# Four scheduling edits in the fourth layer of a four-layer attention stack

## What is computed

```python
zxbcdt = _rms(x, norm_w) @ in_proj_w
z, xBC = zxbcdt[..., :D_INNER], zxbcdt[..., D_INNER:D_INNER + CONV_DIM]
dt = jax.nn.softplus(zxbcdt[..., -H_M:] + dt_bias)
xBC = jax.nn.silu(conv_b + sum((padded[:, k:k + L, :] * conv_w[:, k] for k in range(D_CONV))))
xh, Bm, Cm = ...                       # 8 heads of 64, states of 128
def step(h, inp):                      # over the 112 tokens
    dec, u, bt, ct = inp
    h = h * dec[:, :, None, None] + u[..., None] * bt[:, None, None, :]
    return h, jnp.einsum('bhpn,bn->bhp', h, ct)
y = ys + D_skip[None, None, :, None] * xh
h = x + _rms(y * jax.nn.silu(z), gnorm_w) @ out_proj_w
q, k, v = _ln(h) @ Wq, enc @ Wk, enc @ Wv                    # 8 heads of 32
p = jax.nn.softmax(where(pad_mask, -1e9, q @ k.T / sqrt(32)))
out = h + (p @ v) @ Wo
```

## Time and profile before

| | us |
|---|---|
| median of three runs | 3705.43 |
| the profiled execution | 3712.93 |
| its span, first to last instruction | 3711.1 |
| the fourth layer within it, from 3106 on | 605 |
| TensorE busy over the span | 3461.5 |
| mean granted TensorE clock over the span | 0.966 of full |

### The profile page before, as it was taken

One profiled execution on the slowest core, in us unless ns is written; L12 is line 12 of the kernel. 1 busy time (PEld: TensorE's weight loads), 2 busy tenths in 40 slices (PEclk: granted clock), 3 DMA queues, 4 the chain that ended last, 5 costly groups with the idle time before them and its releaser, 6 DMA issues. The chain is left out here.

```text
span 3711.1 us, 67817 instructions
## 1 busy us (share of the span) xinstructions
PE 3461.5 (93%) x21748; PEld 2540.5 (68%) x21748; DVE 1933.5 (52%) x5863; ACT 1853.4 (50%) x5421; POOL 404.5 (11%) x488
## 2 busy tenths in 40 slices
PE   8999999999988999999979999999999997888888
PEld 6778778778866666666656766667667664555665
DVE  3654644654544444444544544544554545566656
ACT  3543544544445555555545555545545552444444
POOL 2101101101101111111010000000000001112111
PEclk9999999999998999999989999999999997898999
DMA  6000000000004000000010000000000000000000
GB/s 204 4 12 15 4 12 15 4 12 15 4 21 131 14 13 13 13 8 5 13 53 8 9 8 15 9 8 15 8 8 14 9 3 14 22 16 13 13 26 5
DMA packets 58462, 75.11 MB, mean 20 GB/s; under 512 B 6752, under 2 KB 55584, under 8 KB 57024
## 3 DMA queue, kind: packets, MB, share of 16 engines
q1 hardware_dynamic: 58176, 71.45, 6.3%
HBM read 64.04 MB, written 7.40 MB: 19 GB/s over the span
## 5 line engine op out<-in xcount | busy, mean ns | idle before, releaser
L161 PE MATMUL l_bank<-l_xT,weights_of_layers_and 128*128 128x224 f32 x2816 | 622.0, 374 | 18.7 <-ACT l_xT L1137 8.0
L161 PEld LDWEIGHTS l_bank<-l_xT,weights_of_layers_and 128*128 128x128 f32 x2816 | 546.4, 201 | 65.6 <-ACT l_xT L1137 8.7
L387 ACT ACTIVATE l_pT<-l_bank 125x336 f32<-125x336 f32 (+2 forms) x736 | 347.0, 471 | 339.5 <-PE l_bank L319 329.2
L319 PEld LDWEIGHTS l_bank<-identity,l_p 112*125 112x125 f32 (+2 forms) x2336 | 334.8, 178 | 185.6 <-issue 98.1
L319 PE MATMUL l_bank<-identity,l_p 112*125 112x112 f32 (+2 forms) x2336 | 390.1, 279 | 22.8 <-DVE l_p L363 18.5
L404 ACT ACTIVATE l_p<-l_p,l_nm 112x375 f32<-112x375 f32 x384 | 233.4, 608 | 287.2 <-DVE l_nm L438 285.9
L161 PE MATMUL l_bank<-weights_of_layers_and,l_cT 128*125 128x256 f32 (+2 forms) x960 | 303.3, 454 | 11.4 <-DVE l_queries_or_hidden L1839 9.3
L161 PE MATMUL l_bank<-l_cT,weights_of_layers_and 128*128 128x375 f32 x832 | 305.6, 497 | 0.0
L704 POOL TENSOR_TENSOR l_ve<-l_mv,eps 112x2 f32<-112x2 f32 (+1 forms) x89 | 17.3, 195 | 2434.7 <-DVE l_mv L698 2434.7
L363 DVE TENSOR_SCALAR l_p<-l_p,l_rs 112x375 f32<-112x375 f32 (+1 forms) x608 | 256.4, 422 | 21.7
L400 ACT ACTIVATE l_p<-l_p,l_nm 112x112 f32<-112x112 f32 x512 | 192.2, 377 | 150.7 <-DVE l_nm L434 131.9
(11 more groups left out here) (252 smaller groups left out, 5790.3 us busy)
## 6 DMA issues: line engine op xcount, KB each, us to landing
l_cT<-in_ctx_turned SPq DMA_DIRECT2D x32, 375.0 KB, 3.5
l_cx<-in_ctx SPq DMA_DIRECT2D x16, 375.0 KB
context_rows<-in_ctx_reversed SPq DMA_DIRECT2D x16, 375.0 KB
tokens<-x_after_layer SPq DMA_DIRECT2D x25, 224.0 KB, 2.6
x_after_layer<-l_z SPq DMA_DIRECT2D x24, 224.0 KB, 2.4
weights_of_layers_and<-bias_lines_kept SPq DMA_DIRECT2D x1, 2625.0 KB, 16.2
weights_of_layers_and<-in_L_xattn_w_fused SPq DMA_DIRECT2D x1, 2048.0 KB, 10.9
weights_of_layers_and<-in_L_xattn_w_ff SPq DMA_DIRECT2D x1, 2048.0 KB, 12.9
```

What stands on the lines that cost most here:

```text
L161: last = pe.matmul(out, left, right, start=(k == 0), stop=(k == len(pairs) - 1))
L319: last = pe.transpose(TR.bank(m)[:ph.keys, g * ph.rows:(g + 1) * ph.rows], p[:ph.rows, m % self.p_slots, g * ph.keys:(g + 1) * ph.keys], i ...
L387: return act.activation(out, src, ACT.Copy)
```

## The change

Four things change, all in the fourth layer.

1. The 16 row scalings of a turn (`scale`) are done by ScalarE with an ACTIVATE Copy whose scale is the column of inverses, in step n for item n-1, after the exponent of item n. VectorE keeps the inversion.
2. The normalized tokens yT are turned in two jobs, yT0 and yT1, one for each half of the features. The ring has 33 jobs a turn where it had 32.
3. The decays, scans and weighings move: dc00 and dc01 from step 6 to 7, dc10 and dc11 from 8 to 10; the scan of sequence 0 from step 7 to 8, behind the silu, that of sequence 1 from 9 to 11; its weighing from 11 to 10, that of sequence 1 stays in 12, now behind the keys.
4. The square sums of the next tokens move from step 10 to 7; the keys ck00 and ck01 from step 10 to 11, their copy on VectorE from 10 to 12.

```diff
--- before.py
+++ after.py
@@ -359,7 +359,9 @@
         c = ph.col0 + k * ph.n
         eng.wait_ge(self.inverted.sem, self.inverted.count(i, m))
         own = self.p[:r, m % self.p_slots, 0:ph.n * ph.keys * ph.tiles]
-        if ph.n == 1 and ph.scaled_by == "dve":
+        if ph.scaled_by == "act":
+            eng.activation(own, own, ACT.Copy, scale=self.rs[:r, c:c + 1]).then_inc(self.scaled["act"].sem, 1)
+        elif ph.n == 1 and ph.scaled_by == "dve":
             eng.tensor_scalar(own, own, self.rs[:r, c:c + 1], None, ALU.mult).then_inc(self.scaled["dve"].sem, 1)
         else:
             own = own.rearrange("p (g t) -> p g t", g=ph.n)
@@ -414,7 +416,11 @@
             if ph.emptied_by == "act" and ph.closes(k):
                 self.output(act, i, ph, k, copy)
 
-        self.lagged(parts, [(0, amid), (self.lag_t, turned), (0, exps), (self.lag_v, outputs)], between, amid)
+        def scaled(ph, k):
+            if ph.scaled_by == "act":
+                self.scale(act, i, ph, k)
+
+        self.lagged(parts, [(0, amid), (self.lag_t, turned), (0, exps), (1, scaled), (self.lag_v, outputs)], between, amid)
 
     def vector(self, dve, i, parts, between=None, amid=None):
         S, p, nm, sums, rs = self.S, self.p, self.nm, self.sums, self.rs
@@ -2613,13 +2619,13 @@
 
         cross = Part("c", PAIR * H3, DH3, T, cross_q, lambda k, g: ckT[:, cross_at(k)[0], cross_at(k)[1] // 4, :], cross_value, cross_ready, cross_values_ready,
                      lambda k: (f"cO{cross_at(k)[0]}", cross_at(k)[1] // 4 * T), lambda k: OT_of[:, cross_at(k)[0], :], bias=lambda k: padded[:T, :],
-                     sides=4, emptied_by="act")
+                     sides=4, emptied_by="act", scaled_by="act")
         LAST = cross.items + LAG_VALUES
         state_jobs = {-1: [("xT", "act")], 0: [("b0", "act"), ("b1", "act")], 1: [("b2", "act"), ("dt", "dve")], 2: [("z0", "dve")], 3: [("z1", "dve")],
-                      6: [("dc00", "dve"), ("dc01", "dve")], 8: [("dc10", "dve"), ("dc11", "dve")], 9: [("xh0", "act"), ("xh1", "act"), ("g", "act")],
-                      10: [("ck00", "dve"), ("ck01", "dve")], 12: [("ys0", "dve")], 13: [("ys1", "dve")], 14: [("cv00", "act")], 15: [("cv01", "act")],
+                      7: [("dc00", "dve"), ("dc01", "dve")], 9: [("xh0", "act"), ("xh1", "act"), ("g", "act")], 10: [("dc10", "dve"), ("dc11", "dve")],
+                      11: [("ck00", "dve"), ("ck01", "dve")], 12: [("ys0", "dve")], 13: [("ys1", "dve")], 14: [("cv00", "act")], 15: [("cv01", "act")],
                       16: [("uT0", "act"), ("uT1", "act"), ("ck10", "dve")], 17: [("h0", "dve"), ("h1", "dve")], 18: [("ck11", "dve")],
-                      19: [("cv10", "act"), ("yT", "act")], LAST: [("cv11", "act"), ("cq", "act")]}
+                      19: [("cv10", "act"), ("yT0", "act"), ("yT1", "act")], LAST: [("cv11", "act"), ("cq", "act")]}
         out_jobs = {14: [("o0", "dve")], LAST + 1: [("o1", "dve")]}
 
         def names(s):
@@ -2843,13 +2849,13 @@
                     time_steps(i)
                 elif s in (2, 3):
                     gate_rows(i, s - 2)
-                elif s in (6, 8):
-                    decays_spread(i, (s - 6) // 2)
+                elif s in (7, 10):
+                    decays_spread(i, (s - 7) // 3)
                 elif s == 9:
                     for j in range(PAIR):
                         inner_turned(i, j)
                     meetings(i)
-                elif s == 10:
+                elif s == 11:
                     for t in range(KT):
                         context_keys(i, 0, t)
                 elif s in (12, 13):
@@ -2867,10 +2873,15 @@
                     context_keys(i, 1, 1)
                 elif s == 19:
                     context_values(i, 1, 0)
-                    turn_tokens(pe, c, P, i, "yT", xhat, normed.this(1))
+                    for t in range(KT):
+                        for sem, count in P.free(i, f"yT{t}", normed.this(1)):
+                            pe.wait_ge(sem, count)
+                        for j in range(PAIR):
+                            last = pe.transpose(P.bank(f"yT{t}")[:, j * T:(j + 1) * T], xhat[:, j, t * 128:(t + 1) * 128], c.ident[:T, :T])
+                        last.then_inc(P.full.sem, 1)
                 elif s == LAST:
                     context_values(i, 1, 1)
-                    project(pe, P, i, "cq", [columns(V["wq"], t) for t in range(KT)], xT, P.got("yT"))
+                    project(pe, P, i, "cq", [columns(V["wq"], t) for t in range(KT)], xT, P.got("yT1"))
 
             def output(i, j):
                 rows_of(f"o{j}", i, lambda kt: OT[:, j, kt, :], lambda kt: V["wo"][:, kt, :], D, O.got(f"cO{j}"))
@@ -2958,11 +2969,10 @@
                         last.then_inc(P.emptier(f"uT{j}").sem, 1)
                 elif s == 19:
                     context_values(i, 1, 0)
-                    act.wait_ge(P.full.sem, P.count_full(i, "yT"))
                     for t in range(KT):
-                        last = act.activation(xT[:, t, :], P.bank("yT")[:, t * TP:(t + 1) * TP], ACT.Identity, scale=c.column["L3_ca_ln_w"][:, t:t + 1],
-                                              bias=c.column["L3_ca_ln_b"][:, t:t + 1])
-                    last.then_inc(P.emptier("yT").sem, 1)
+                        act.wait_ge(P.full.sem, P.count_full(i, f"yT{t}"))
+                        act.activation(xT[:, t, :], P.bank(f"yT{t}")[:, 0:TP], ACT.Identity, scale=c.column["L3_ca_ln_w"][:, t:t + 1],
+                                       bias=c.column["L3_ca_ln_b"][:, t:t + 1]).then_inc(P.emptier(f"yT{t}").sem, 1)
                 elif s == LAST:
                     context_values(i, 1, 1)
                     act.wait_ge(P.full.sem, P.count_full(i, "cq"))
@@ -3058,7 +3068,7 @@
             def weigh(i, j):
                 if j == 0:
                     dve.wait_ge(P.emptier("g").sem, P.count_emptied(i, "g"))
-                    dve.wait_ge(P.emptier("dc11").sem, P.count_emptied(i, "dc11"))
+                dve.wait_ge(P.emptier(f"dc{j}1").sem, P.count_emptied(i, f"dc{j}1"))
                 for half in range(2):
                     own = decays[:, 2 * j + half, :].rearrange("p (g t) -> p g t", g=G)
                     dve.tensor_tensor(own, own, wide(score[:, j, :], 1, G), ALU.mult).then_inc(weighted.sem, 1)
@@ -3096,18 +3106,19 @@
                 elif s == 6:
                     conv_tap(i, 2, range(TILES))
                 elif s == 7:
-                    scanned(i, 0)
+                    measure_x(i + 1)
                 elif s == 8:
                     dve.wait_ge(conv_tanh.sem, conv_tanh.count(i, 0))
                     dve.scalar_tensor_tensor(conv, th, 1.0, conv, ALU.add, ALU.mult).then_inc(conv_silu.sem, 1)
-                elif s == 9:
+                    scanned(i, 0)
+                elif s == 10:
+                    weigh(i, 0)
+                elif s == 11:
                     scanned(i, 1)
-                elif s == 10:
+                elif s == 12:
                     for t in range(KT):
                         keys_kept(i, 0, t)
-                    measure_x(i + 1)
-                elif s in (11, 12):
-                    weigh(i, s - 11)
+                    weigh(i, 1)
                 elif s in (13, 14):
                     gate_state(i, s - 13)
                 elif s == 15:
```

## The result

The changed kernel takes 3681.62 us, median of 5 runs (3680.68 to 3682.54), where 3705.43 stood; the ratio is 0.9925 with an interval of 0.9914 to 0.9935. 3698.5 had been forecast with a range down to 3684: right in sign, a good quarter of the size (6.9 us of 23.8). One thing is needed to read the traces: executions of the kernel before fall into two groups, 3703.7 to 3707.8 and 3711 to 3714.7, and its profiled ones lie in the upper one, so that trace against trace shows 32 us and not 24.

What follows compares the result with a forecast made beforehand. In full turns DVE bounds the middle, PE most of the rest; the last turn is a three-engine loop. Full turns -10.5, first pass -1.0, last turn +4.6 give -6.9 us from 3705.43: 3698.5 us, range 3684 to 3712.

Steps and rivals of the forecast that it cites:

- middle stretch: Steps 3 to 9 of a full turn, DVE without a gap and PE waiting: score products to end 3.4 us earlier.
- Turn start: Start of each turn: tokens' transposes reuse cv11's bank, ACT's idle 0.77 us can go; 0.8 us taken, bounds 0 to 0.8.
- Tanh as the silu's releaser: Full turn: silu 2.4 us earlier, released by ACT's tanh, with DVE idle 0.9 us before it.
- The decays of sequence 1 back to back on PE with no wait: Full turn, between scores and the context's keys: these decays run on PE without waiting; 2.3 us charged.
- signs named for being wrong: Full turns no shorter or over 3 us shorter; sequence 0's weighing over 2 us; last turn unchanged; differences outside fourth layer.
- the value of a scaling: Row scalings leaving DVE: 0.33 us each where DVE is the bound, four counted before the last convolution tap.
- POOL's penalty on the taps: Convolution taps on DVE meet 2.5 us of POOL's work instead of 1.0; 1.2 us charged.
- What the last stretch takes back: Score products to turn end, PE the bound: moved decays cost 2.3 us, leaving 1.1 net of 3.4 at ys1.
- Rival C: Full turns: POOL's products delay sequence 0's weighing, over about 2 us late decides; slower, 3717 us; chance 0.13.
- Rival A: Full turns: whole gain stays, taps slowed by POOL no more than before, PE holds its clock; 3687 us; chance 0.28.
- First pass: Fourth layer's opening pass without attention: silu no longer waits for a scan; 1 us gained, between -1 and 4.
- Last turn: Closing attention-only turn: scaling on ACT lengthens the two-step loop from 2.45 to 3.14 us; 4.6 us lost, 3.0 to 5.5.

Runs made afterwards that it cites:

- the fastest kernel: Kernel before with the scalings by ScalarE and yT in two jobs, old order kept, the last turn's scalings left to VectorE: 3665.94 us, ratio 0.9881.

## Why the prediction was wrong

**Right.** The seat of the change (middle stretch and last turn). Turn start: 0.8 taken, ScalarE's xT is 0.74 earlier after (2.20 us of the turn instead of 2.94), and with part 2 turns go from 67.9 to 67.2 at clock 0.95. Tanh as the silu's releaser, DVE idle 0.9 before it: 0.90. The decays of sequence 1 back to back on PE with no wait. The signs of the full and the last turn. Two of the signs named for being wrong came: turns shorter by over 3 us, and a weighing of over 2 us.

A full turn gained 3.4 us at like clock, where 1.5 stood. The 1.9 us between them lie in three terms of the sum: 0.5, 0.6 and 0.8.

**The step that failed first is the value of a scaling: "0.33 is what one is worth where DVE is the bound".** I read it between the scaling's start and what follows. But the scaling also waits for the reciprocal. DVE of the seventh turn, before and after:

```profile
3621.05 0.16 DVE L450 RECIPROCAL l_rs<-l_sums 112x1 f32<-112x1 f32 x1
3621.24 0.42 DVE L363 TENSOR_SCALAR l_p<-l_p,l_rs 112x375 f32<-112x375 f32 x1
3621.57 0.17 DVE L3035 TENSOR_SCALAR l_r<-l_e 112x16 f32<-112x16 f32 x1
```
```profile
3585.84 0.16 DVE L456 RECIPROCAL l_rs<-l_sums 112x1 f32<-112x1 f32 x1
3585.91 0.16 DVE L3045 TENSOR_SCALAR l_r<-l_e 112x16 f32<-112x16 f32 x1
```

From the reciprocal's start to the next work: 0.52 us before, 0.07 after. One scaling is worth 0.45. In the four steps that I counted up to the last convolution tap this makes 0.5 us more.

**POOL's penalty on the taps**, 1.2 charged: the six taps took 3.69 instead of 3.08 us, 0.6; POOL's own spreading in turn took 3.71 instead of 4.58 with fewer DVE operations beside it. With the scalings' 0.5 this is the whole error of the middle stretch: the last tap ends 2.4 us earlier and not 1.3, and the score products end 4.5 earlier and not 3.4.

**"What the last stretch takes back", 2.3 us**: ys1 starts 3.0 us earlier (46.3 instead of 49.3 us of the turn), where I had 1.1. So 1.5 was taken back, not 2.3. The mechanism was the right one: PE has the decays where it is the bound, as parts 1 and 2 with the old order show by contrast. Behind ys1 I had another 0.4, and about as much came (3.0 to 3.4). Rival C's mechanism was there (the weighing at 2.22, above its mark of 2), but in this kernel the slack took it up. Rival A's 3.1 was nearest to the 3.4, by luck: its reason was that POOL would slow the taps no more than before, and it slowed them by 0.6.

**First pass**, 1 gained: 5.6 in the traces, of which 0.9 is its earlier start. PE's busy time there fell from 48.66 to 41.41 us with the same 172 instructions: most is clock (0.71 to 0.80). The other traces show what the order has in it. Counted from its first transposes, the first pass takes 60.2 to 60.5 us in five kernels with the old order (clock 0.71 or 0.72), 57.7 to 57.9 in the other four (0.75 or 0.76), and 55.4 to 55.7 in all nine with the new one (0.80 to 0.83). So the order is worth 2 to 5 us here, depending on which of the two lengths it replaces, where I had 1. What decides between these two is not shown.

**Last turn**, +4.6 taken, +5.7 measured: right mechanism, and the loop of the right size. After (start, us):

```profile
3648.31 0.61 ACT L406 ACTIVATE l_p<-l_p,l_nm 112x375 f32<-112x375 f32 x1 [0.40 <-DVE l_nm L444]
...
3648.92 0.59 ACT L363 ACTIVATE l_p<-l_p,l_rs 112x375 f32<-112x375 f32 x1
3649.41 0.43 ACT L389 ACTIVATE l_pT<-l_bank 125x336 f32<-125x336 f32 x1
3649.74 0.60 ACT L406 ACTIVATE l_p<-l_p,l_nm 112x375 f32<-112x375 f32 x1
```

The scaling takes 0.59 (0.57 estimated), and two steps take 3.16 us, as against 3.14 in the sum and 2.45 before. The last exponent starts 27.6 us into the turn instead of 24.1, 3.5 later. The other 2.2 lie behind it, where the clock fell. The last 10 us of the turn, before and after:

```profile
3701.00:3711.10 10.10, 5.31 (x66) 3.42 (x66) 2.33 (x9) 3.00 (x9) 0.00 (x0) 1.00 0.08 23
```
```profile
3668.80:3678.90 10.10, 4.63 (x36) 2.82 (x34) 0.59 (x2) 2.82 (x8) 0.00 (x0) 0.62 0.08 23
```

In them the output projection takes 2.02 us after and 1.09 before, the values ahead of it 1.35 and 0.78. The sum had no term for the clock here. DVE for the last turn brings 32.5 us back.

**Sum.** By the traces: seven turns 32.3, first pass 5.6, less 5.7: 32.2 us. Of the turns' 32.3, 24.0 are seven times the 3.4 of the seventh turn, and 8.3 are there because other turns of the profiled execution before were longer, at clocks of 0.86 to 0.93. From the median the gain is 23.8 us, 8.4 less than by the traces: the profiled execution before took 7.5 us more than its median, the one after 0.9 less than its own. My sum of 6.9 is some 17 short of it: 13.5 in the full turns (24.0 for 10.5), 4.6 in the first pass, less 1.1 in the last turn. Part 1 carries the turns; parts 3 and 4, by themselves worth 6 to 7 us by their ratio, through the first pass and the clock, cost 7.5 to 8.8 on top of it.

## What to carry to other kernels

- Find the last operation of the waiting engine that the turn depends on (here a weighing), and price what stands ahead of it on that engine. It counts in full only where that engine runs without a gap (here from step 3 to the second scan); ahead of its idle stretches it gave little (0.3 us for two scalings), and behind the last operation nearly nothing (0.15 us for four). The sizes of single waits on TensorE do not tell: cutting the largest in half moved it to the next.
- Work moved from a stretch in which an engine waits to one in which it does not is paid for there: the decays, 2.2 us long, cost PE 1.5 us a turn in their new place.
- The price of a small dependent operation is read from its predecessor's start with it and without it (0.52 and 0.07 us here), not from its own start to the next.
- Moving work to an engine with room helps in turns where that engine is not in the loop, and hurts where it is; the last turn can have another division.

## What was not expected of the hardware

- The same kernel, without an edit, shows full turns of 71.5 and 74.6 us in the same places in two profiled executions, with the same instructions at a granted clock of 0.93 and 0.86; PE was busy 60.1 and 63.4 us. In the fastest kernel four of seven turns take 65.5 us, at 0.97 to 1.00, and three take 67.2 at 0.95. Edits worth 1 us a turn are mixed with such shifts, so single turns were compared at the nearest clock there was.
- Two weighings of 448 columns (DVE tensor by tensor) take 1.15 us alone and 2.0 to 2.85 beside POOL's products. The Trainium skill ("GPSIMD Engine Reference", Specifications) names shared SBUF interfaces for this case; the trace agrees in kind, with a factor of 1.8 to 2.5.
- A multiplication of 112 x 375 by a constant holds DVE 0.25 us before the next operation starts, one by a column of reciprocals just made 0.33 us and 0.12 us of wait ahead of it.
